# Turning the split rows of each node tile: TensorE products against one transposing transfer per tile

## The reference, cut to what matters

```
x = ln(x + gcn(x))     # x @ W.T, normalised sum over edges, batch norm, gelu, + x
x = ln(x + sage(x))    # twice: relu(h @ W_self + mean over edges(h) @ W_neigh + b)
x = ln(x + rgcn(x))    # twice: sum over edges of sigmoid(gate) * x[col] @ w[r], w[r] mixed from 30 bases, + x @ root + bias
x = ln(x + gin(x))     # relu((h + sum over edges(h)) @ W1 + b1) @ W2 + b2
```

## Time and profile before

| what | value |
|---|---|
| median of 3 runs | 1015.59 us (1014.8 to 1017.13) |
| the profiled execution's own time | 1016.28 us |
| its span in the profile | 1014.5 us |
| TensorE busy with products | 967.5 us, 95% of the span |
| VectorE busy | 669.1 us, 66% |
| ScalarE busy | 365.7 us, 36% |
| granted TensorE clock, mean | 0.99 |

### The profile page before, as it was taken

How to read it: one execution, slowest core, us unless ns; L and a number is a source line. 1 busy time by engine, 2 the same in 40 slices (tenths; PEclk the granted TensorE clock), 3 DMA queues, 4 the chain that set the end, 5 groups by cost and what they waited for, 6 DMA issues and landing times.

```text
span 1014.5 us, 15078 instructions
## 1 busy us (share of the span) xinstructions
PE 967.5 (95%) x4904; PEld 472.2 (47%) x4904; DVE 669.1 (66%) x1262; ACT 365.7 (36%) x520; POOL 85.2 (8%) x66
## 2 busy tenths in 40 slices
PE   6899999998999799998999899999999999999997
PEld 2444444444555554444444344444444444445443
DVE  5776767664243767999999999999233334542258
ACT  0224344545587442344313322111632231144342
POOL 1000011111011100210211100000400010010000
PEclk9999999999999899999999999999999999999999
DMA  8634443444211115565553155551001003110014
GB/s 276 231 116 132 131 123 114 145 135 126 95 42 43 52 55 195 163 217 191 169 174 102 64 158 146 175 145 53 1 21 42 1 22 114 63 42 1 1 52 154
DMA packets 59445, 108.59 MB, mean 107 GB/s; under 512 B 6497, under 2 KB 6966, under 8 KB 59386
## 3 DMA queue, kind: packets, MB, share of 16 engines
q1 hardware_dynamic: 38522, 68.45, 22.0%
q10 hardware_dynamic: 20864, 39.33, 11.9%
HBM read 95.24 MB, written 12.52 MB: 106 GB/s over the span
## 4 chain that ended last, share of the span: by engine, by line
PE 78%; DVE 14%; DMA 3%; issue 2%; ACT 2%; POOL 1%; DVEq 0%; ACTq 0%; SPq 0%
PE Dp L610 25%; PE Dp L637 23%; PE T L551 11%; PE Dp L512 10%; PE Dp L662 4%; DVE acc L1128 4%; PE T L584 2%; PE T L535 1%; DVE stt L1219 1%; PE Dp L672 1%; DVE Zraw L1238 1%; DVE w L1256 1%; DMA Zraw<-in_basis 1%; DVE mcol L1082 1%; DVE acc L1283 1%
## 5 line engine op out<-in xcount | busy, mean ns | idle before, releaser
L610 PE MATMUL Dp<-W,hT 128*128 128x512 f16 x1320 | 296.9, 381 | 5.9 <-ACT hT L821 4.6
L610 PEld LDWEIGHTS Dp<-W,hT 128*128 128x128 f16 x1320 | 127.0, 98 | 150.9 <-ACT hT L821 6.6
L637 PE MATMUL Dp<-Zraw,A 128*128 128x512 f16 x800 | 173.3, 379 | 0.0
L1128 DVE SCALAR_TENSOR_TENSOR acc<-stage,att,acc 128x512 f32<-128x512 f32 x232 | 168.1, 792 | 1.4 <-DMA stage<-in_basis 1.4
L637 PE MATMUL Dp<-Zraw,AT 128*128 128x512 f16 x600 | 130.8, 379 | 0.5 <-DVE Zraw L1196 0.5
L551 PE MATMUL T<-Zraw,W 128*128 128x512 f32 x240 | 114.6, 615 | 10.8 <-DVE W L1011 8.5
L637 PEld LDWEIGHTS Dp<-Zraw,A 128*128 128x128 f16 x800 | 78.2, 98 | 93.9
L512 PE MATMUL Dp<-Zraw 128*128 x594 | 111.6, 343 | 3.9 <-issue 3.3
L1056 DVE TENSOR_SCALAR Zraw<-hT,w 128x1280 f16 x198 | 102.7, 561 | 0.0
L821 ACT ACTIVATE hT<-T 128x1024 f16<-128x1024 f32 x70 | 71.5, 1021 | 85.0 <-PE T L584 80.1
L1050 DVE SCALAR_TENSOR_TENSOR Zraw<-w,hT 128x256 f16 x99 | 49.8, 503 | 65.4 <-PE Dp L512 46.6
(11 more groups left out here) (158 smaller groups left out, 772.2 us busy)
## 6 DMA issues: line engine op xcount, KB each, us to landing
Zraw<-in_basis SPq DMA_DIRECT2D x120, 256.0 KB, 3.0
stage<-in_basis SPq DMA_DIRECT2D x120, 256.0 KB, 2.9
xres<-w ACTq DMA_DIRECT2D x30, 256.0 KB, 2.0
xr<-xres ACTq DMA_DIRECT2D x30, 256.0 KB, 2.6
wst<-in_Wn ACTq DMA_DIRECT2D x4, 1024.0 KB, 5.6
wst<-in_Ws ACTq DMA_DIRECT2D x4, 1024.0 KB, 5.5
wst<-mixd ACTq DMA_DIRECT2D x4, 1024.0 KB, 5.4
wst<-in_root ACTq DMA_DIRECT2D x3, 1024.0 KB, 6.1
```

Of the source, the lines that this page charges most:

```text
L610: last = nc.tensor.matmul(Dp[:, j, m, :], hT[:, j, hp, k * P:(k + 1) * P], weights_of(u, m)[:, wp, k, :], start=(n == 0), stop=(n == 3 * K ...
L637: last = nc.tensor.matmul(sum_bank(t), a[:, k, ds(t * P, P)], Z[:, r, h, k, :], start=(n == 0), stop=(n == count - 1))
L1128: last = v.scalar_tensor_tensor(part, stage[:, q, :], a, part, ALU.mult, ALU.add)
```

## The change

Each tile is turned by one DMA that transposes, issued from ScalarE's queue, from S16 to hT. `turn` and `hT_out` are gone, and with them the semaphore s_t; s_hT becomes four semaphores, one for each buffer. Units with one matrix (0, 5, 6) now have four buffers (two of them in a part of Zraw that is free in these units), the others two. `turn_to(end)` issues the transfers in the order of the tiles: each waits for s_ready of its tile and for s_d of the tile that last read the buffer. In z_out(t) it is called up to tile t-1 plus the number of buffers, from t = 1 on. The first two tiles of the next unit are issued at steps 3 and 4 of the relu or layer norm steps; in units 0, 5 and 6 tiles 2 and 3 (and in unit 0 all four) are issued before the first z_out.

```diff
-        s_t = sem("s_t")
-        s_hT = sem("s_hT")
+        s_hT = [sem(f"s_hT{i}") for i in range(4)]
...
+        hT_far = Zraw[:, 2 * NT * D:2 * NT * D + 4 * D].rearrange("p (a h d) -> p a h d", a=2, h=2)
+        HT_ORDER = [(u, t) for u in range(NU) for t in range(NT)]
+        def hT_ring(u):
+            return 4 if len(UNITS[u]["mats"]) == 1 else 2
+        def hT_slot(u, t):
+            i = t % hT_ring(u)
+            return i, hT[:, i] if i < 2 else hT_far[:, i - 2]
+        def hT_users(u, t):
+            mine = hT_slot(u, t)[0]
+            return [a for a in HT_ORDER[:HT_ORDER.index((u, t))] if hT_slot(*a)[0] == mine]
...
                 def dense(t, j):
-                    if nm == 1 and t < NT - 1:
-                        turn(t + 1, 1 - j)
-                    pe.wait_ge(s_hT, t + (NT * u + 1))
+                    slot, turned = hT_slot(u, t)
+                    pe.wait_ge(s_hT[slot], 16 * (len(hT_users(u, t)) + 1))
...
-                        if nm > 1 and m == 0 and t < NT - 1:
-                            turn(t + 1, 1 - j)
...
-                    if u and isinstance(t, int) and t == NT - 2:
-                        turn(0, 0, u + 1)
...
-                if u < 2:
-                    turn(0, 0)
...
-                def hT_out(t, j, u=u):
-                    act.wait_ge(s_t, t + (NT * u + 1))
-                    wait(act, s_d, t + (NT * u - 1))
-                    nc.scalar.activation(hT[:, j, :, :], T[:, :, :], ACT.Copy).then_inc(s_hT, 1)
+                def turn_to(end, u=u):
+                    while turned[u] < min(end, NT):
+                        t = turned[u]
+                        slot, out_tile = hT_slot(u, t)
+                        act.wait_ge(s_ready, NT * u + t + 1)
+                        if hT_users(u, t):
+                            before, tile = hT_users(u, t)[-1]
+                            act.wait_ge(s_d, NT * before + tile + 1)
+                        if slot == 2 and u == 5 and t == 2:
+                            act.wait_ge(s_agg[4], NT)
+                        act.dma_start_transpose(out_tile.rearrange("p h (k n) -> p (h k) n", k=KT),
+                                                S16[:, t, :]).then_inc(s_hT[slot], 16)
+                        turned[u] += 1
...
                 def ln_step(t, j):
-                    if t == NT - 2 and u == 4:
-                        hT_out(0, 0, u + 1)
-                    if t == NT - 1:
-                        hT_out(1, 1, u + 1)
                     deviation(t, j)
-                    if t == NT - 3 and u == 2:
-                        hT_out(0, 0, u + 1)
+                    if t > 2:
+                        turn_to(min(t - 2, 2), u + 1)
...
                 def z_out(t, j):
-                    if not (t == NT - 1 or t == 0 and u in (2, 3, 4, 5) or u == 1 and t < 5):
-                        hT_out(t + 1, 1 - j)
+                    if t:
+                        turn_to(t + hT_ring(u))
...
                 if u == 0:
-                    hT_out(0, 0)
+                    turn_to(2)
...
+                if hT_ring(u) == 4:
+                    turn_to(4)
...
                 def relu_step(t, j):
-                    if t == NT - 2:
-                        hT_out(0, 0, u + 1)
-                    if t == NT - 1 and u in (1, 3):
-                        hT_out(1, 1, u + 1)
+                    if t > 2:
+                        turn_to(min(t - 2, 2), u + 1)
...
                         if t == 1:
-                            hT_out(0, 0, 1)
+                            turn_to(1, 1)
...
                         if t in turned_after and t != 1:
-                            hT_out(turned_after[t], turned_after[t] % 2, 1)
+                            turn_to(turned_after[t] + 1, 1)
                         if t == 2:
-                            hT_out(1, 1, 1)
+                            turn_to(2, 1)
```

More of the change, by code:

```diff
@@ L609, in dense @@
                             for k in range(KT):
-                                last = nc.tensor.matmul(Dp[:, j, m, :], hT[:, j, hp, k * P:(k + 1) * P],
+                                last = nc.tensor.matmul(Dp[:, j, m, :], turned[:, hp, k * P:(k + 1) * P],
                                                         weights_of(u, m)[:, wp, k, :], start=(n == 0), stop=(n == 3 * KT - 1))
@@ L684, in _ @@
                 if u == 0:
-                    pe.wait_ge(s_hT, NT)
                     pe.wait_ge(s_zlo[0], NT - 1)
@@ L813, in _ @@
             nc.scalar.activation(dinv[:, :], dinv[:, :], ACT.Sqrt).then_inc(s_dsq, 1)
+            turned = [0] * NU
             for u, unit in enumerate(UNITS):
                 nz = unit["nz"]
-                def hT_out(t, j, u=u):
-                    act.wait_ge(s_t, t + (NT * u + 1))
-                    wait(act, s_d, t + (NT * u - 1))
-                    nc.scalar.activation(hT[:, j, :, :], T[:, :, :], ACT.Copy).then_inc(s_hT, 1)
+                def turn_to(end, u=u):
[11 more added lines that the diff above has]
+                        turned[u] += 1
                 def load_residual(t, j):
```

## The result

The changed kernel takes 1023.13 us in the median of 5 runs (1021.93 to 1026.36), the kernel before 1015.59 us (1014.8 to 1017.91, 5 runs): ratio 1.0076, 95% interval 1.0054 to 1.0099. The forecast was 1008 us. The measured time lies inside the range, but on the other side of no change. Two of the runs behind this document, one of the kernel before (1717.87 us) and one of a later experiment (3513.67 us), were in a slow state, and the medians are of the others. The profiled execution has a span of 1021.3 us against 1014.5 before, and a mean granted TensorE clock of 0.972 against 0.990.

The account below looks back on a forecast made before the run. TensorE was taken to bound the kernel (967.5 of 1014.5 us busy), with VectorE as full or fuller from 407 to 563. Stage terms summed to -7.4 us against 1016.3: 1008.9, median 1008.2, forecast 1008; range 993 to 1046.

Parts of the forecast that it names:

- it lands at 6.6 against 5.18: +1.4 twice: Unit 1 to 407 us: transfers just behind a 1 MB load land after the two-step allowance; +1.4 us each of two times.
- the budget of 5.18 us: Two-matrix units with two buffers: a transfer must land within 2 x 2.59 = 5.18 us.
- From 407 until unit 3's third tile starts at 583: 0: There, time saved from 22 tile transposes on TensorE goes into its wait for VectorE: 0 us.
- the nine turns of unit 1: Unit 1's dense stage: TensorE's transposes of nine tiles go, five for -2.2 us and four for -1.8.
- its -3.1: Unit 3's dense stage: seven tile transposes go, -3.1 us; VectorE's 7.28 us a tile, under TensorE's 7.77, does not stop it.
- The turns' own price: All stages: transposing one tile of eight blocks costs TensorE 0.45 us; seventy are 31 us, the most that could be won.
- The hold: Time ScalarE's sequencer is occupied issuing one transposing transfer: taken as 2.6 us, as eight plain issues.
- the landing: Transposing transfer from start of issue to arrival: taken as 4.3 us, 2.6 for issuing and about 1.7 more.
- The start: Unit 0: sequencer free at 249.6, first transfer lands at 253.9, where products began at 252.58: +1.3 us.
- the -1.5 up to unit 1's first products: Unit 0's nine tile transposes go, -4.0 us; unit 1's tile 0 lands at 346.9 against products at 344.42, +2.5.
- The long hold: Rival: issuing occupies ScalarE 3.9 us, so one-matrix units run at ScalarE's pace; +25, 1041 us; chance 0.27.
- Slow landing: Rival: transfers cheap to issue but arriving after 7.5 us; two-matrix units wait 2.3 us a tile; 1033 us; chance 0.09.

Follow-up runs that it names:

- small loads: Changed kernel with unit 2's and later weight loads and all gate loads cut to 16 of 128 partitions, order unchanged: 1005.79 us, one run.
- transfers a stage earlier: Changed kernel with transfers issued ahead of the loads, and third tiles (unit 5 also fourth) before the preceding aggregation's last step: 1003.81 us, ratio 0.9883.
- the loads moved on top: Kernel with transfers a stage earlier, plus the weight loads of units 2 and 3 issued from SyncE's queue: 1006.90 us, ratio 0.9913.
- the small basis: Changed kernel with SyncE's second basis transfers, all but the first four, cut to 16 of 128 partitions: 1018.5 us, one run.

## Why the prediction was wrong, step by step

Spans of the profiled executions; the differences forecast and measured, in us, each rounded.

| step | forecast | measured |
|---|---|---|
| start, to unit 0's first products | +1.3 | -0.4 |
| from there to unit 1's first products | -1.5 | -1.5 |
| unit 1's dense stage to unit 3's third tile | -1.2 | +17.2 |
| rest of unit 3's dense stage | -3.1 | -1.2 |
| aggregations 3 and 4, unit 4 | -4.9 | -4.9 |
| unit 5 | +2.4 | -0.7 |
| aggregation 5, unit 6 and the end | -0.4 | -1.6 |
| together | -7.4 | +6.8 |

**The step that failed** is the third row, in two of its terms. The first is unit 1's "it lands at 6.6 against 5.18: +1.4 twice". I had the place, a transfer issued just behind a load of 1 MB, and took the load's 5.6 us plus 1 us for the transfer. Measured, the two transfers (376.57 and 401.66) land in 10.2 and 6.2 us, and TensorE waits 6.02 and 3.52 us: 9.5 where the term had 2.8. In the first case the load took 7.0 us beside the other traffic and the transfer landed another 3.7 behind it. In the second the forecast landing was nearly right (6.9 us from the load's issue), but that load was issued 1.7 us after the part of Z before it, which the budget of 5.18 us did not allow for. Unit 1 from its first products took 9.5 us more (62.6 to 72.1), where -1.2 was forecast.

The second term is "From 407 until unit 3's third tile starts at 583: 0". It came out at +7.7 (176.0 to 183.7 us). I stopped looking for loads there, because VectorE's lag would cover whatever came; it took the gain, but not the waits of 10.16 and 6.19 us behind transfers that land in 9.3 and 10.8. The loads ahead of the transfers of 469.14 and 499.22 stand in the kernel's PREP list for anyone who reads it against the new issues. The gate loads, two issues of 256 KB, were left out too: the transfer behind them took 10.6 us, though TensorE, late already, did not wait for it.

The rest of this row was not sound either. Without its two load terms it says -4.0, the nine turns of unit 1. With small loads unit 1 gained 2.6 us (62.6 to 60.1), and the way from there to unit 3's third tile lost 1.9 of them (176.0 to 177.9): -0.7. Three kernels without that harm (small loads 237.9 us, transfers a stage earlier 239.0, with the loads moved on top 238.1) take the stretch in 237.9 to 239.0 us, against 238.6 before. So VectorE takes back unit 1's gain as well, and not only that of the turns behind 407.

**The clock** was in no term. Behind the waits of 3.52 to 10.16 us TensorE starts below full clock (0.50 from 598 to 601); unit 3's dense stage lost about 1.9 us that way (0.97 over 64.1 us), which is why its -3.1 came out as -1.2. In units 1 and 2 the four groups behind such waits take 7.1 us more than as many products at full clock (17.54 for 72 against 15.70, for one). The 3.2 us wait in unit 5 shows both cases: the 24 products behind it take 5.34 us in the changed kernel and 8.22 in the one with the small basis.

**The turns' own price held.** Unit 4 and the turns around it gave -4.9 where eleven times 0.45 us was forecast. It is the one stage in which TensorE is the only bound, before and after.

**The hold and the landing** were both too high (2.6 and 4.3 against 1.25 and 3.0). The start gained 0.7 us by that and 1.0 because the first issue was at 248.6, not 249.6; in unit 5 TensorE waits 3.19 us after the second tile, not 5, and then takes 2.59 us a tile, not 2.7. In unit 6 VectorE sets the pace in both kernels (3.04 and 2.97 us a tile), so the 1.2 us more than forecast there are not shown to come from the hold. And the -1.5 up to unit 1's first products was met by luck: unit 0's dense stage gave 2.8 us instead of 4.0, and the way from its end to unit 1's first products cost 1.3 us instead of 2.5. Eight blocks were read as eight issues; the trace has one of 1.25 us, and half of the blocks hold as long.

**The rivals.** The long hold, put at 0.27, is refuted. Slow landing, put at 0.09, had the mechanism nearest to what happened, waits of TensorE for landings in the two-matrix units, but for another reason: a transfer of 1056 packets of about 250 bytes lands in 3.0 us when alone. With the measured waits of 9.5 us instead of 2.8, unit 1's two transfers alone would have taken the forecast to 1015, no change, before unit 2 is counted. The sign was wrong because the cheap parts were argued one by one, while this one got one sentence and a cover.

## What to carry to other kernels

A DMA that takes over work from a busy engine inherits the traffic of its queue: list every load that stands ahead of it, in each stage, and price the landing as the load's own plus the transfer's, both under that stage's traffic, against the slack that the buffers give. Issue the short urgent transfer before the long one that can wait, and one stage early where the engine that issues it may itself be late; here the two together turned +0.8% into -1.2%. Tell a transfer that lands late from one that is issued late: a quarter of the waits in the changed kernel were of the second kind. A stage bound by another engine covers waits only up to that engine's lag, and a wait of some us costs TensorE clock on top.

## What was unexpected of the hardware

- A transposing transfer of 128 by 1024 float16 holds ScalarE's sequencer for 1.25 us in the median (3.00 at most), one of half the size for 1.30 us, against 0.327 us for a plain issue.
- It lands in 3.0 us when alone, a plain store of the same bytes in 2.0; it is 1056 packets, and took (0.219 x 1021.3 - 0.119 x 1014.5) x 16 = 1647 us of the DMA engines for 73920 packets, 22 ns each, where queue 1's are 93 ns for 1.8 KB. The Trainium skill ("VectorE: DVE Perf Modes", The three transpose paths) has 1309 ns for one such block by DMA; eight blocks in 3.0 us show that its figure does not add up by blocks.
- Behind a load of 1 MB it lands in up to 10.8 us. With the load in the other queue it landed once in 4.9 us (the load 2.6 us ahead), but still in 9.8 and 10.8 where two loads of 256 KB stand ahead in its own.
